# Spreading ahead of the small work in each slot, joined norm rows, and transpositions in two 64-row halves

## What is computed

```python
def _L0_conv_ref(x, Wk, bk, Wq, bq, Wv, bv, Wr, br, head_count):
    k = jax.nn.relu(_conv1x1(x, Wk, bk).reshape(B, head_count, hk, N))
    q = jax.nn.relu(_conv1x1(x, Wq, bq).reshape(B, head_count, hk, N))
    v = _conv1x1(x, Wv, bv).reshape(B, head_count, hv, N)
    context = jnp.einsum('bhkn,bhvn->bhkv', k, v)
    attended = jnp.einsum('bhkv,bhkn->bhvn', context, q)
    return _conv1x1(attended.reshape(B, Cv, H, W), Wr, br)
def _L0_ffn_ref(x, router_w, router_b, expert_w, expert_b):
    router_probs = jax.nn.softmax(x @ router_w + router_b, axis=-1)
    top_p, top_i = jax.lax.top_k(router_probs, K)
    top_p = top_p / jnp.sum(top_p, axis=-1, keepdims=True)
    expert_out = jnp.einsum('bnd,edc->bnec', x, expert_w) + expert_b
    gathered = jnp.take_along_axis(expert_out, top_i[..., None], axis=2)
    return jnp.einsum('bnk,bnkc->bnc', top_p, gathered)
x = x + _L0_conv_ref(_ln_c(x), ...)      # layer norm over the 64 channels
t = _to_tokens(x)
t = t + _L0_ffn_ref(_ln_t(t), ...)       # norm over the channels, 8 experts, best 2
```

## Time and profile before

| | us |
|---|---|
| median of three runs | 705.34 (703.17 to 705.6) |
| the profiled execution | 708.03 |
| its span, first to last instruction | 706.2 |
| PE busy | 647.4 (92%) |
| DVE busy | 532.2 (75%) |
| ACT busy | 428.5 (61%) |
| POOL busy | 396.5 (56%) |

### The profile page before, as it was taken

The page is one execution under the profiler, slowest core; times in us unless marked ns, Lnnn a source line. Parts: engine busy times, 40 slices in busy tenths (PEclk is TensorE's granted clock), DMA queues, the critical chain, the costliest instruction groups (busy, mean ns, idle before and its releaser), DMA issues.

```text
span 706.2 us, 20616 instructions
## 1 busy us (share of the span) xinstructions
PE 647.4 (92%) x7846; PEld 302.0 (43%) x7846; DVE 532.2 (75%) x1176; ACT 428.5 (61%) x852; POOL 396.5 (56%) x350
## 2 busy tenths in 40 slices
PE   3898999799999999999999999999989889896786
PEld 1676766444544444444544444444322223231221
DVE  3443456878788988888788988867889998978853
ACT  2354556857566676657576776756656666564542
POOL 7132342165456566565456566555657667575785
PEclk9999999999999999999999999999999999999999
DMA  6232544655565555555566564444656555454442
GB/s 141 61 75 71 130 122 122 169 145 123 136 151 135 136 140 125 127 136 123 133 150 148 123 148 99 98 111 107 149 130 152 120 120 135 102 131 97 107 104 46
DMA packets 32660, 86.16 MB, mean 122 GB/s; under 512 B 7650, under 2 KB 7826, under 8 KB 32562
## 3 DMA queue, kind: packets, MB, share of 16 engines
q1 hardware_dynamic: 32082, 84.64, 50.7%
q0 software_dynamic: 288, 0.19, 0.1%
q10 hardware_dynamic: 192, 0.01, 0.0%
HBM read 34.47 MB, written 16.78 MB: 73 GB/s over the span
## 4 chain that ended last, share of the span: by engine, by line
PE 68%; DVE 13%; ACT 10%; issue 7%; DMA 1%; POOL 1%; DVEq 0%; SPq 0%; ACTq 0%; POOLq 0%
PE bank L1073 25%; PE bank L1059 8%; PE bank L986 5%; PE bank L921 5%; PE bank L974 5%; PE bank L943 4%; PE bank L911 4%; ACT grows L565 3%; DVE z L816 3%; PE bank L1020 3%; PE bank L1006 2%; ACT L543 2%; DVE osb L826 2%; PE bank L1070 2%; DVE x L720 2%
## 5 line engine op out<-in xcount | busy, mean ns | idle before, releaser
L431 POOL TENSOR_TENSOR z<-gbs,x1d 128x512 f32<-128x512 f32 x256 | 320.6, 1275 | 220.7 <-ACT gbs L571 164.8
L1076 PE MATMUL bank<-z,ew 128*64 128x512 f32 x512 | 248.0, 607 | 0.0
L1073 PE MATMUL bank<-z,ew 128*64 128x512 f32 x512 | 247.9, 607 | 0.0
L571 ACT COPY gbs<-bank 128x512 f32<-128x512 f32 x256 | 140.0, 593 | 95.3 <-PE bank L1059 94.4
L816 DVE TENSOR_TENSOR z<-bank,x1d 128x512 f32<-128x512 f32 x256 | 162.9, 677 | 20.4 <-PE bank L1059 20.1
L1059 PE MATMUL bank<-grows,sel 64*64 64x512 f16 x1024 | 89.3, 388 | 28.2 <-DVE z L816 17.0
L422 POOL TENSOR_TENSOR xsq<-xin 128x512 f32<-128x512 f32 x64 | 65.6, 1046 | 81.8 <-DMA xin<-in_x_dram 78.2
L1073 PEld LDWEIGHTS bank<-z,ew 128*64 128x64 f32 x512 | 65.7, 138 | 105.6 <-issue 95.8
L492 ACT COPY xn<-bank 128x512 f32<-128x512 f32 x64 | 34.6, 588 | 68.2 <-PE bank L921 68.2
L676 DVE TENSOR_TENSOR xnT<-bank,rstd 128x512 f32<-128x512 f32 x64 | 41.3, 684 | 39.2 <-PE bank L911 37.0
L1059 PEld LDWEIGHTS bank<-grows,sel 64*64 64x64 f16 x1024 | 24.1, 104 | 97.2 <-issue 34.4
(11 more groups left out here) (138 smaller groups left out, 885.0 us busy)
## 6 DMA issues: line engine op xcount, KB each, us to landing
x1d<-x SPq DMA_DIRECT2D x128, 256.0 KB, 4.5
xin<-in_x_dram SPq DMA_DIRECT2D x64, 256.0 KB, 4.1
x_again<-in_x_dram SPq DMA_DIRECT2D x64, 256.0 KB, 4.1
out_dram<-osb SPq DMA_DIRECT2D x128, 128.0 KB, 2.4
k<-in_const_dram SPq DMA_DIRECT2D x1, 453.5 KB, 3.7
ew_nat<-in_L_ffn_expert_w_dram POOLq DMA_DIRECT2D x2, 64.0 KB, 6.5
sel<-in_const_sel_dram SPq DMA_DIRECT2D x1, 128.0 KB, 3.5
bk_rows<-bk_wide ACTq DMA_DIRECT2D x6, 1.0 KB, 1.7
```

The source lines that it names most:

```text
L431: pool.tensor_tensor(z[:, 1, i % R_Z, :], gbs[:, i % R_Z, :], x1d[:, g % 2, 1, u * NT:(u + 1) * NT], ALU.mult).then_inc(z_pool, 1)
L571: nc.scalar.copy(gbs[:, i % R_Z, :], bank[:, :]).then_inc(taken_of(("spread", i, 1)), 1)
L1073: pe.matmul(out_bank[0:C, :], ew[:, j, :], z[:, 0, i % R_Z, :], start=False, stop=(j == PAIRS - 1), skip_group_check=True).then_inc(prod_d ...
L1076: pe.matmul(out_bank[C:P, :], ew[:, j, :], z[:, 1, i % R_Z, :], start=False, stop=(j == PAIRS - 1), skip_group_check=True).then_inc(prod_d ...
```

## The change

- Each slot begins, on all engines, with the spreading and its products and copies; the small work comes after it, and on PE the experts last. DVE's `result` therefore comes after the slot's products.
- The norm rows of x (group n) and of x1 (group n - 12) go into one bank, one 128 x 256 copy and two transpositions instead of four; the weights put them in different rows. The column and gate transpositions move to slot 1, ahead of turning back, and the sums come last in that slot.
- Experts run 18 steps behind instead of 17, gate rows 17 instead of 16; x1 has eight buffers instead of seven. The 27 gate steps are cut at other places and begin two slots later.
- Turning x and back: sixteen transpositions of 64 rows by 128 columns instead of eight of 128 x 128, alternating between the upper and the lower 64 rows; each half writes to a bank of its own. `normalise` and `take_back` then read a half `s` or `h` each, instead of a stretch `u`.
- `bank_uses` lists the uses in the new order (not shown).

```diff
-L_COLS, L_TURN, L_KEYS, L_AGAIN, L_ATTEND, L_ROUTE, L_GATES, L_TURN_GATES, L_EXPERTS = 1, 2, 3, 9, 11, 12, 14, 16, 17
+L_COLS, L_TURN, L_KEYS, L_AGAIN, L_ATTEND, L_ROUTE, L_GATES, L_TURN_GATES, L_EXPERTS = 1, 2, 3, 9, 11, 12, 14, 17, 18
...
-R_X, R_Q, R_X1, R_Z = 3, 8, 7, 4
+R_X, R_Q, R_X1, R_Z = 3, 8, 8, 4
...
-        for k, col in enumerate((0, S, SE, SE + S)):
+        for k, col in enumerate((NLG, NLG + S, SE, SE + S)):
...
-            p, late = divmod(SLOTS * (n - L_GATES) + k - 1 - phase, 2 * SLOTS)
+            p, late = divmod(SLOTS * (n - L_GATES) + k - 3 - phase, 2 * SLOTS)
...
+            def take_back(g, h):
+
...
+                nc.scalar.copy(xn[:, g % 2, :].rearrange("p (a h n) -> p a h n", h=2, n=C)[:, :, h, :],
+                               bank[:, :].rearrange("p (a n) -> p a n", n=C)).then_inc(taken_of(("back", g, h)), 1)
...
+            def take_rows(n):
+
+                bank = when_filled(act, ("rows", n, 0))
+                nc.scalar.copy(rows_sb[:, :, :].rearrange("p u n -> p (u n)"), bank[:, 0:U * P]
+                               ).then_inc(taken_of(("rows", n, 0)), 1)
+
+            def take_cols(n):
+
+                bank = when_filled(act, ("cols", n, 0))
+                columns = bank[:, 0:U * P].rearrange("p (a r) -> p a r", r=W)
+                g = n - L_ROUTE
+                if real(g):
+                    upto(act, gate_dve, (g // 2 - 2) * N_GATE + 8)
+                    half = g % 2 * U * NJ
+                    ins = nc.scalar.copy(lg[:, g // 2 % 2, half:half + U * NJ, :], columns[:, :, 0:NLG])
+                if real(n):
+                    upto(act, xstat_dve, n * N_XSTAT)
+                    ins = nc.scalar.copy(xs[:, :, :], columns[:, :, NLG:NROW])
+                ins.then_inc(taken_of(("cols", n, 0)), 1)
 
             def root_x(g):
...
-            gate_steps = {0: root_dev, 5: exponent, 7: high, 8: low}
+            gate_steps = {0: root_dev, 4: exponent, 7: high, 8: low}
...
                 for k in range(SLOTS):
+                    for i in iterations(n, k + 1):
+                        copy_gates(i)
+
                     if k == 0:
                         if real(n - L_KEYS):
                             for s in range(S):
                                 take_keys(n - L_KEYS, s)
-                        if real(n - L_COLS):
-                            take_stat_cols(n - L_COLS)
-                        if real(n - L_ROUTE - L_COLS):
-                            take_route_cols(n - L_ROUTE - L_COLS)
-                    if k == 1 and real(n - L_TURN):
-                        for u in range(U):
-                            take_back(n - L_TURN, u)
-                    if k == 3:
+                    if k == 1:
+                        if has_rows(n - L_COLS):
+                            take_cols(n - L_COLS)
                         if real(n - L_TURN_GATES):
                             take_gate_rows(n - L_TURN_GATES)
-                        if real(n):
-                            take_stat_rows(n)
-
-                    for i in iterations(n, k + 1):
-                        copy_gates(i)
-
-                    if k == 1 and real(n - L_COLS):
-                        root_x(n - L_COLS)
-                    if k == 2 and real(n - L_KEYS):
-                        for s in range(S):
-                            take_queries(n - L_KEYS, s)
+                        if real(n - L_TURN):
+                            for h in range(2):
+                                take_back(n - L_TURN, h)
+                    if k == 2:
+                        if real(n - L_COLS):
+                            root_x(n - L_COLS)
+                        if real(n - L_KEYS):
+                            for s in range(S):
+                                take_queries(n - L_KEYS, s)
                     if k == 3:
-                        if real(n - L_ROUTE):
-                            take_route_rows(n - L_ROUTE)
                         if real(n - L_ATTEND):
                             for u in range(U):
                                 square_x1(n - L_ATTEND, u)
+                        if has_rows(n):
+                            take_rows(n)
                     for phase, step in gate_steps.items():
                         if quad_in(n, k, phase) is not None:
                             step(quad_in(n, k, phase))
...
+            def normalise(g, s):
...
+                dve.tensor_tensor(xnT[:, g % 2, :, :, 1 + C * s:1 + C * s + C].rearrange("p u j c -> p (u j) c"),
+                                  bank[:, :].rearrange("p (a c) -> p a c", c=C),
+                                  rstd[:, g % 2].rearrange("p u (j s) -> p (u j) s", s=S)[:, :, s].unsqueeze(2)
+                                  .to_broadcast([P, U * NJ, C]), ALU.mult
+                                  ).then_inc(taken_of(("turned", g, s)), 1)
...
-            gates_by_phase = {8: (26, 27), 0: (0, 4), 2: (4, 9), 3: (9, 12), 4: (12, 16), 6: (16, 20), 7: (20, 26)}
+            gates_by_phase = {8: (26, 27), 0: (0, 4), 1: (4, 8), 2: (8, 13), 4: (13, 16), 5: (16, 18), 6: (18, 24), 7: (24, 26)}
...
                 for k in range(SLOTS):
+                    for i in iterations(n, k + 1):
+                        product(i)
+
                     if folding(n, k):
                         fold(*folding(n, k))
                     if k == 0 and real(n - L_EXPERTS - 1):
                         result(n - L_EXPERTS - 1, 1)
-                    if k == 1:
-                        if real(n - L_KEYS):
-                            add_sums(n - L_KEYS)
-                        if real(n - L_COLS):
-                            x_deviations(n - L_COLS, 0, 4)
+                    if k == 1 and real(n - L_KEYS):
+                        add_sums(n - L_KEYS)
                     if k == 2:
                         if real(n - L_EXPERTS):
                             result(n - L_EXPERTS, 0)
                         if real(n - L_ATTEND):
                             for u in range(U):
                                 residual(n - L_ATTEND, u)
-                    if k == 3 and real(n - L_COLS):
-                        x_deviations(n - L_COLS, 4, N_XSTAT)
                     for phase, (k0, k1) in gates_by_phase.items():
                         if quad_in(n, k, phase) is not None:
                             gates(quad_in(n, k, phase), k0, k1)
                     if k == 0 and real(n - L_TURN):
-                        for u in range(U):
-                            normalise(n - L_TURN, u)
-
-                    for i in iterations(n, k + 1):
-                        product(i)
+                        for s in range(S):
+                            normalise(n - L_TURN, s)
+                    if k == 1 and real(n - L_COLS):
+                        x_deviations(n - L_COLS, 0, 4)
+                    if k == 3 and real(n - L_COLS):
+                        x_deviations(n - L_COLS, 4, N_XSTAT)
...
+            def turn_x(g):
+
+                uses = [("turned", g, s) for s in range(S)]
+                banks = [when_free(pe, use) for use in uses]
+                for a in range(U * NJ):
+                    for s in range(S):
+                        rows = slice(C * s, C * s + C)
+                        ins = pe.transpose(banks[s][:, a * C:(a + 1) * C], xin[rows, g % R_X, a * P:(a + 1) * P],
+                                           eye[rows, rows])
+                        if a == U * NJ - 1:
+                            ins.then_inc(filled_of(uses[s]), 1)
+
+            def turn_back(g):
+
+                uses = [("back", g, h) for h in range(2)]
+                banks = [when_free(pe, use) for use in uses]
+                for s in range(S):
+                    when_taken(pe, ("turned", g, s))
+                for a in range(U * NJ):
+                    for h in range(2):
+                        rows = slice(C * h, C * h + C)
+                        ins = pe.transpose(banks[h][:, a * C:(a + 1) * C],
+                                           xnT[rows, g % 2, a // NJ, a % NJ, 1:P + 1], eye[rows, rows])
+                        if a == U * NJ - 1:
+                            ins.then_inc(filled_of(uses[h]), 1)
...
+            def make_rows(n):
+
+                use = ("rows", n, 0)
                 bank = when_free(pe, use)
-                outs = [bank[W * j:W * (j + 1), 0:U * P].rearrange("p (u n) -> p u n", u=U) for j in range(NJ)]
-                for moving, weights, start in ((tile, w, True), (squares, w_square, False)):
-                    chunks = moving.rearrange("p (u j n) -> p u j n", u=U, j=NJ)
+                parts = []
+                if real(n):
+                    pe.wait_ge(x_in[n % R_X], 32 * (n // R_X + 1))
+                    pe.wait_ge(x_squared, (n + 1) * U)
+                    parts += [(xin[:, n % R_X, :], mean_w), (xsq[:, :], square_w)]
+                g = n - L_ROUTE
+                if real(g):
+                    pe.wait_ge(x1_squared, (g + 1) * U)
```

(51 more changed lines are left out.)

92 lines of the change are left out of this document (20 added, 72 removed).

## The result

| | before | after |
|---|---|---|
| median | 705.5 us (4 runs) | 782.5 us (780.9 to 784.2, 4 runs) |
| ratio | | 1.109, 95% interval 1.104 to 1.114 |
| span of the profiled execution | 706.2 | 779.0 |
| step 16's norm rows begin at | 139.6 | 142.7 |
| from there to step 17's | 19.1 | 17.5 |

The account below looks back on a forecast made before the run. The prediction took PE to bound the kernel (busy 19.38 of a 19.70 us step), DVE second. From 706.2, fill +3, added step +5.6, joint part +13.3 and drain +14 gave 742, stated as 741 for the median; range 690 to 765.

Parts of the forecast that it names:

- (c): DVE's small SBUF steps stand still while POOL multiplies, 1.02 and 1.19 instead of 0.18; placed in even slot 3, odd slot 0.
- (b): Slot 1: late PE sums hold DVE in `add_sums`, with gate steps, deviations and products queued behind; slot 2 stalls 1.2 to 1.8.
- PE's work: Pieces of PE's work per step: 17.8 together, 1.9 less than now, with each turning at 0.46 instead of 0.87.
- (a): Slots 0 and 2: bias matmul waits for `result` behind two products; level in joint part, drain gains 1.65 and 0.85.
- the rival built on that, 767: Turning x and back: the halves don't run side by side and stay at 0.87, adding 25 to 742; chance 0.08.
- (d): Odd slot 0: ACT's copies wait behind its root and low-part copies; turning x's bank is free at 3.0, PE ready at 1.7.
- One more step: Experts 18 steps behind: a fill step of 9.5 and a drain step of 15.9 come, one of 19.75 goes: +5.6.
- The rest of the fill: Fill: turning back waits for both normalised halves behind only 0.37 of column work, 7.0 for 6.74 a step, about +3.
- keep its pace: Rival: DVE's queue has slack and the stalls don't add up; a step is 18.1, total 692; chance 0.22.
- The cancelling case (705): Rival: gains and stalls cancel, joint mean near 19.0 and level drain, with (b) stalling PE under 0.5; chance 0.10.

Follow-up runs that it names:

- e4: The changed kernel with DVE's `result` put ahead of the products in slots 0 and 2: 760.8 us, ratio 1.081 to the kernel before.
- e6: The changed kernel with PE's sums put first among slot 1's small work: 737.0 us, ratio 1.044 to the kernel before.
- e13: The changed kernel with DVE's deviations of x moved behind the residual in slot 2: 757.1 us, ratio 1.076 to the kernel before.
- e7: The changed kernel with POOL's products cut to 32 of 512 columns, leaving out part of the output: 735.5 us, ratio 1.042 to the kernel before.
- e5: The changed kernel with DVE's gate steps of slot 1 moved ahead of `add_sums`: 741.2 us, ratio 1.050 to the kernel before.
- e10: The changed kernel with `result` ahead of the products in slots 0 and 2 and PE's sums first in slot 1: 711.2 us, ratio 1.010.
- e1: The kernel before with only the turning changed to sixteen 64-row transpositions, `take_back` and `normalise` going with it: 702.2 us, ratio 0.996.
- e9: The changed kernel with the attention matmuls issued twice, in front of PE's wait in slot 2: 787.7 us, ratio 1.119 to the kernel before.
- e2: The changed kernel with turning, `take_back` and `normalise` put back to the 128-row form: 768.9 us, ratio 1.092 to the kernel before.
- e14: The changed kernel with 128-row turning put back and POOL's products cut to 32 of 512 columns, leaving out part of the output: 736.1 us, ratio 1.044.

## Why the forecast was wrong, and where it was right

Two steps of it failed. It had VectorE's held-up steps (c) in the wrong slots: the runs show them between the sums and slot 2's products of every second step, 2.7 us in place of the 0.83 that (b) had. And it put TensorE's clock at nothing, which cost 1.4 to 2.8 us in four of those steps.

**PE's work: right in kind.** On after's PE timeline sixteen transpositions of 64 rows cost 0.64 with a change of shape in it (the second start minus the first):

```profile
411.15 0.71 PE L901 MATMUL bank<-k,xin 64*128 64x64 f32 x16 [0.17 <-ACT gbs L563]
411.79 0.41 PE L1066 MATMUL bank<-grows,eb_rows 128*64 128x512 f16 x2
```

Less the 0.14 this is 0.50, and turning back is the same, 0.63 (416.17 to 416.80), with the change to the sums' shape in it: 0.46 was a little short, 0.87 is out. By the Trainium skill (TensorE: Matmul & The Clock Gate, section LDWEIGHTS (loading the stationary operand)) a load of 128 columns takes 107 ns, so eight groups one behind the other would take 0.86, an estimate. The trace disagrees for these transpositions, and the rival built on that, 767, is refuted as a mechanism, though the number is nearer to the result.

**(a), bias behind `result`: right, undersized in the drain.** The drain was forecast at 270.3 + 15.9 + 14 = 300 for 18 steps and took 309.9. e4 takes out 29.7 there, 1.65 a step. On the PE timeline the wait is 2.65 in slot 0 of a drain step, where DVE's gate steps in front were held up by POOL (0.76 and 1.20 for two of them):

```profile
567.43 0.64 PE L1066 MATMUL bank<-grows,eb_rows 128*64 128x512 f16 x2 [2.65 <-DVE osb L815]
```

Slot 0's 1.65 was that of an undisturbed DVE: in the next drain step it is 1.76 (584.79). In slot 2 it is 1.05 and 1.15 where 0.85 was said. The expert pairs behind the 2.65 come 0.86 apart (567.86, 568.72), so the lower clock costs here too. The sum should have had both in it: 9.7 missing.

**(b), sums last in slot 1: right, and the largest.** `add_sums` waits 1.29 and 1.47 where 1.3 was said, and e6 gets back 45.5. The queries wait 0.72 and 3.07 where 1.2 to 1.8 was said, though.

**(c), DVE's steps behind POOL: right as a mechanism, applied in the wrong slots.** The deviations entered (b) at 0.83 in every step. The collisions were placed in slots 3 and 0, and in (b) only at one gate step of the even steps (L796, here L785, 0.49). In the second step of a pair, DVE has six gate steps between the sums and the deviations, and these arrive just as POOL starts: 2.7 from the first of them to the products (440.20 to 442.88), 0.8 in the first step (420.34 to 421.13). e13 moves them out and gets 25 us, e7 shortens POOL and gets 47. These gains and e6's 45.5 overlap and can't be added, since each edit also shifts when VectorE meets POOL. This is the step that failed.

**The clock: a term put at nothing.** With the wait of over 3 us came the lower clock. The second steps with that wait are alike but for it: 21.75 in the one with a clock of 1.00, 24.5 and 24.4 at 0.86, 23.2 and 23.3 at 0.93. That is about 8 us in these four. In the pair without it (20.14 and 21.75) the error of (c) and that of (d) below nearly cancel: 41.9 where 41.5 was forecast. Joint: 20.7 forecast, 22.1 measured, 19.1 missing.

The Trainium skill (SBUF — State Buffer, section Who interferes with whom) says that VectorE and GpSimd share one pair of ports, that the pair is an exclusive lock, and that a VectorE instruction wants it when it has two inputs in SBUF or is in a two-port mode. The trace agrees: the held steps end with POOL's two instructions, 441.46 and 442.67 where the pair has its middle at 441.41 and its end at 442.65, and steps on PSUM banks beside POOL keep their 0.42. One of the two held steps, L644, has a single input; in which mode it ran no trace shows.

**(d), copies delayed before turning x: mostly absent.** In the first of the two steps above PE waits 0.17 before turning x, where 1.3 was said (0.40 in the second, where nothing was). The first step of a pair, forecast at 21.6, took 20.1 to 20.8; the second, forecast at 19.9, took 21.8 to 24.6. Two errors of opposite sign; the mean hid a part of them. On the PE timeline of e13 the wait appears, 1.57:

```profile
391.55 0.72 PE L901 MATMUL bank<-k,xin 64*128 64x64 f32 x16 [1.57 <-ACT gbs L563]
```

In e5 and e6 it is 0.71 in these steps (at 379.8 and 374.1), and in e7, where (c) is gone, under 0.25, as the forecast had it.

**One more step: undersized.** The added fill step was priced at 9.5 from PE's pieces and took 17.5. PE waits in it for the whole gate run of a pair on DVE and ACT: 1.83, 1.24 and 1.12 us at the three waits below, on its timeline.

```profile
148.87 0.41 PE L1002 MATMUL bank<-k,rows_sb 128*128 128x128 f32 x2 [1.83 <-ACT rows_sb L497]
150.52 0.61 PE L1041 MATMUL bank<-eye,gT 128*128 128x128 f16 x8 [1.24 <-ACT gT L550]
152.25 1.11 PE L915 MATMUL bank<-k,xnT 64*128 64x64 f32 x16 [1.12 <-DVE xnT L664]
```

Behind them the sums and the attention take 1.96 and 1.76 (153.29, 155.25, 157.01), where joint steps of before show 1.03 and 0.91 (386.69, 387.72; 391.17, 392.08); the clock is 0.80 over this step (window 142.73:160.20). Before, the last fill step already took 13.4 (126.26 to 139.61 by its norm rows), with the same kind of waits. That row was a better one to price it by than PE's pieces, though 4.1 of the 8.0 missing would still be missing. The rest of the fill, +3 forecast, came to +3.1.

The three misses, 8.0 + 19.1 + 9.7, are the 37 us between 742 and 779.0. The range failed because it took its ends from the same walk of the queues; it had no case in which a collision is in the slot with the longest wait, and none for the clock. The forecast's own bounds were also added up wrong: their terms end at 742 + 10 = 752, not 762. The result lies above both.

**The rivals.** PE didn't keep its pace (692), since slot 2 stalled, though not by the amounts said. The cancelling case (705) needed (b) under 0.5; e10, with both waits mended, comes nearest to it with 711. What is left open: the 6 us between e10 and before, of which the added step is the likely part but was not taken out alone; and why (d) is nearly absent in after and present in e13.

## What to carry to other kernels

When an order of work is changed, look for the strictest queue and list, for each wait put into it, everything behind that wait and what the other engines need of it: two edits of a few lines (e4 and e6) are worth 71 of 77 us here, and work saved on the bound engine only 3 (e1). Price a new step by the neighbouring step's measured length rather than by its pieces, and small VectorE steps on SBUF at their held-up duration wherever GpSimd may be working, since tenths of a microsecond decide which it is. A range for a change of order should be wider on the slow side than a walk through the queues gives.

## What the runs showed of the hardware

- Transpositions of 64 rows by 128 columns in the two row halves of the array run side by side: sixteen in 0.63 to 0.64 us with the change of shape behind them (after, 411.15 and 416.17), where eight of 128 rows took 0.97 to 1.03.
- A small f32 step of VectorE on SBUF takes 0.17 to 0.19 alone and up to 1.24 beside a GpSimd product, 1084 ns in the mean of L631. Steps with PSUM operands (0.42, L751 to L781) keep their duration.
- Behind 3.07 us without matmuls the granted clock stayed at 1.00 in one step of five. In another it was 0.81 for 1.7 us and 0.57 for the 3.2 us after that. Behind 2.21 us (e9) it fell in two of five, behind 1.85 us (e2) in none. Such a step was 1.4 to 2.8 us longer, so a wait of TensorE can cost half its length again or more, but need not.
- Of two kernels in the same order, the one with less TensorE work was 14 us slower (after and e2), by phase as far as the runs show: with POOL's products short they are level (735.5 and 736.1, e7 and e14).
